# Where the sixteen matmuls of probabilities and values stand inside a slot

## The reference, cut to what matters

```python
qkv = einsum('bsh,oh->bso', hidden_states, w_qkv)      # 16 heads of 32
scores = einsum('bhqd,bhkd->bhqk', q, k) * scale
scores = where(causal, scores, finfo.min)
probs = softmax(scores, axis=-1)
attn = einsum('bhqk,bhkd->bhqd', probs, v)             # the sixteen matmuls
x = layernorm(x + einsum('bsh,oh->bso', attn, w_o))
```

## Time and profile before

| | |
|---|---|
| median of 3 runs | 2699.21 us (2698.35 to 2701.85) |
| the profiled execution | 2696.95 us, its span 2695.2 us |
| granted TensorE clock, mean | 0.992 |
| PE busy | 2629.0 us of the span, 98% |
| DVE busy | 1554.0 us, 58% |
| ACT busy | 1103.4 us, 41% |
| first and last start of the values' matmuls | 65.8 us and 735.2 us |

### The profile page before, as it was taken

One profiled execution on the slowest core, in us unless ns is written; L12 is line 12 of the kernel. 1 busy time (PEld: TensorE's weight loads), 2 busy tenths in 40 slices (PEclk: granted clock), 3 DMA queues, 4 the chain that ended last, 5 costly groups with the idle time before them and its releaser, 6 DMA issues.

```text
span 2695.2 us, 37715 instructions
## 1 busy us (share of the span) xinstructions
PE 2629.0 (98%) x13314; PEld 2146.4 (80%) x13314; DVE 1554.0 (58%) x3224; ACT 1103.4 (41%) x2518; POOL 827.1 (31%) x992
## 2 busy tenths in 40 slices
PE   7999999999789999999999999999999999999998
PEld 6777887778467888888888888888888888888886
DVE  5777777777788888876333333633333363333334
ACT  4666666666644444443222222322222232222221
POOL 1444444443633443334111111321111132111112
PEclk9999999999799999999999999999999999999999
DMA  8666876768376565556444433554344335433441
GB/s 247 186 181 174 219 211 173 190 187 234 103 257 242 195 223 213 213 203 240 174 172 174 178 141 141 196 218 172 141 173 179 141 155 225 174 141 141 178 174 47
DMA packets 143085, 493.52 MB, mean 183 GB/s; under 512 B 11568, under 2 KB 48560, under 8 KB 118320
## 3 DMA queue, kind: packets, MB, share of 16 engines
q1 hardware_dynamic: 142896, 491.11, 52.9%
HBM read 356.84 MB, written 134.22 MB: 182 GB/s over the span
## 4 chain that ended last, share of the span: by engine, by line
PE 70%; DVE 2%; DMA 1%; issue 1%; POOL 0%; ACT 0%; SPq 0%; POOLq 0%; DVEq 0%; ACTq 0%
PE bank L1035 23%; PE bank L1036 23%; PE bank L1037 23%; DMA scale<-up_scales 0%; PE bank L448 0%; DMA scale<-down_scales 0%; PE bank L434 0%; DMA x1T_scratch<-x_late 0%; POOL probs L736 0%; DVE bstats L1483 0%; DVE acc L1426 0%; DVE w_d L1399 0%; SPq L915 0%; PE bank L415 0%; PE bank L458 0%
## 5 line engine op out<-in xcount | busy, mean ns | idle before, releaser
L1645 POOL TENSOR_TENSOR inter_l<-hid,inter_h 128x512 fp32r<-128x512 f32 x256 | 339.2, 1325 | 1366.8 <-ACT inter_h L1166 1366.8
L1426 DVE TENSOR_TENSOR acc<-acc,bank 128x512 f32<-128x512 f32 x512 | 350.3, 685 | 331.6 <-PE bank L1037 322.6
L1035 PE MATMUL bank<-wd,inter_h 128*128 128x512 f32 x1024 | 399.7, 390 | 8.1 <-DVE acc L1426 7.1
L1037 PE MATMUL bank<-wd,inter_l 128*128 128x512 f32 x1024 | 398.9, 390 | 0.0
L1036 PE MATMUL bank<-wd,inter_h 128*128 128x512 f32 x1024 | 398.9, 390 | 0.0
L736 POOL TENSOR_SCALAR probs<-probs,row_inv 128x128 f32<-128x128 f32 (+3 forms) x512 | 264.5, 538 | 365.8 <-DVE row_inv L657 365.8
L1445 DVE TENSOR_TENSOR hid<-hid,bank 128x512 f32<-128x512 f32 x192 | 132.0, 687 | 398.9 <-PE bank L1037 397.2
L1035 PE MATMUL bank<-bx_h,wg 128*128 128x512 f32 x896 | 349.3, 390 | 4.2 <-ACT bank L1166 3.2
L1036 PE MATMUL bank<-bx_l,wg 128*128 128x512 f32 x896 | 348.7, 389 | 0.0
L1037 PE MATMUL bank<-bx_h,wg 128*128 128x512 f32 x896 | 348.6, 389 | 0.0
L1037 PE MATMUL bank<-bx_h,wu 128*128 128x512 f32 x896 | 348.6, 389 | 0.0
(11 more groups left out here) (139 smaller groups left out, 4355.0 us busy)
## 6 DMA issues: line engine op xcount, KB each, us to landing
wg<-w_scratch SPq DMA_DIRECT2D x48, 1792.0 KB, 9.0
wu<-w_scratch SPq DMA_DIRECT2D x48, 1792.0 KB, 12.8
wd<-w_scratch SPq DMA_DIRECT2D x48, 1024.0 KB, 4.9
q_st<-qk_scratch SPq DMA_DIRECT2D x128, 256.0 KB, 5.1
k_st<-qk_scratch SPq DMA_DIRECT2D x128, 256.0 KB, 6.9
w_scratch<-wg SPq DMA_DIRECT2D x16, 1792.0 KB, 9.6
w_scratch<-wu SPq DMA_DIRECT2D x16, 1792.0 KB, 6.0
qk_scratch<-q_stage SPq DMA_DIRECT2D x32, 512.0 KB, 3.6
```

The source lines that it names most:

```text
L1035: pe.matmul(out, a(0), b(0), start=start, stop=False, skip_group_check=True)
L1037: return pe.matmul(out, a(1), b(0), start=False, stop=stop, skip_group_check=True)
L1426: dve.tensor_tensor(a, a, d_bank[n % 2][:, :], ALU.add).then_inc(d_added, 1)
L1645: pool.tensor_tensor(inter[1][:, m, t, :], hid[:, 2 * m + t, :], f32(inter[0][:, m, t, :]), ALU.subtract).then_inc(inter_split, 1)
```

## The change

One number in the PE order: the values are issued in step k = 2 instead of step k = 0. They still stand behind that step's scores and projections and ahead of that step's transposes; the transposes of the first and the second key tile (k = 0 and k = 1) now go ahead of them.

```diff
-                        if v_head and v_head[1] % 4 == 3 and k == 0:
+                        if v_head and v_head[1] % 4 == 3 and k == 2:
                             values(t_use(b, s - 1, 0, cur, prev), v_head[0] // 4, v_head[1] // 4)
                         if t_head:
                             transpose_probs(t_use(b, s, k, cur, prev), *t_head, k)
```

## The result

The changed kernel takes 2739.8 us in the median against 2699.3 before: a ratio of 1.0147, 95% interval 1.0131 to 1.0163. The profiled execution took 2739.65 us, its span 2737.9. One of its four executions took 9388 us and is left out of the ratio. The forecast was 2740, range 2727 to 2749.

A forecast was written before the change was run, and what follows sets the result against it. PE was taken as the bound, busy 85.92 of 86.58 us in a batch. Terms 15.8 + 11.1 + 11.2 + 0 + 2.0 + 0.6 = 40.7 us, added to 2699.2, gave 2740 us; range (8 in 10) 2727 to 2749.

The forecast's parts named there:

- slots 3 and 15 and slot 11 of batch 0: Fifteen slots where third transposes and fourth score come late: 1.05 us each, 15.8 us in all.
- Slot 7: Batches 1 to 7, DVE late from an output projection: 1.59 us each, seven times, 11.1 us.
- Slot 11: Batches 1 to 6, DVE loaded by normings and x1 transposes: 1.86 us each, six times, 11.2 us.
- Odd ones: Slot 7 of batch 0: 0; batch 7: slot 11 2.0 us, slot 15 0.6; slot 3 of batch 8: nothing.
- Wait (a): Third transposes, now right behind the values, wait for DVE's copy of key tile 0: 0.85 us in slot 3.
- Wait (b): Fourth score waits for the mask behind DVE's copy of key tile 0: about 0.2 us, 1.05 later in all.
- The upper bound: 2750 us: 0.2 to 0.3 us more in each of 30 slots for PE's next weights, tail 2 more.
- Slot 11 of batch 7: No projections there; values start only behind the first mask: 0.7 to 2.8 us lost, 2.0 taken.
- ACT's delay at nothing: ACT's waiting copy delays two exponentials and a stage copy; ACT, 41% busy, stood idle there: no cost.
- No loss: Rival: no loss or a gain of 1 to 2 us if pT's space were free; 2698 us, chance 0.05.
- The direct wait alone: Rival: DVE catches up, so only the third transposes' wait for the copy costs; 2724 us, chance 0.11.
- The clock: Rival: each new wait of about 1 us also lowers PE's granted clock; 2803 us, chance 0.04.

The follow-up runs named there:

- e1: Changed kernel (values in step 2) plus a second buffer for the first head of every second group; 2703.2 us, ratio 1.0017.
- e4: Changed kernel, values still in step 2 but ahead of that step's projection matmuls instead of behind them; 2719.6 us, ratio 1.0079.
- e5: Changed kernel, but in slots with values DVE issues the second mask before the copy of key tile 0; 2732.0 us, ratio 1.0124.
- e8: Changed kernel plus the second buffer, values spread: the four matmuls of key tile k stand in step k; 2718.6 us, ratio 1.0077.
- e6: Changed kernel, but values back in step 0 in slot 11 of batch 7 only; 2735.4 us, ratio 1.0137.
- e7: As e1, but second buffer only for key tiles 0 and 2, copied by DVE; ACT's copy of key tile 1 still waits; 2709.1 us, ratio 1.0038.
- e2: Kernel before (values in step 0) plus the second buffer for the first head of every second group; 2697.8 us, ratio 1.0000.
- e3: Changed kernel with the values in step 1 instead of step 2, one buffer; 2705.0 us, ratio 1.0026.

## Why the prediction was right

*The terms.* By its own steps: slots 3 and 15 and slot 11 of batch 0, forecast 15.8, measured 15 times about 1.13, 17.0 us. Slot 7, forecast 11.1, measured 8.3. Slot 11, forecast 11.2, measured 10.4. Odd ones, forecast 2.6, measured 3.5. The sum of the slots is 39.3 against 40.7. The medians differ by 40.5 us, which is nearer to the forecast than the terms deserve: errors of both signs cancelled, and the 1.2 us between 39.3 and 40.5 belong to no term of the sum. Of the signs named, the batch came to 91.70 us against 92.1 forecast, and the waits of L434 for pT (L677) grew by 27.0 us against some 25.

*Wait (a), the third transposes:* forecast 0.85 later than before, measured 0.90 in slot 3 of batch 6 (5.81 us behind the slot's first score before, 6.71 after; the row shows 0.89 as idle time). The copy starts 0.14 behind the values' end (591.96), where 0.03 was reckoned, and the values start 3.46 behind the first score, where 3.52 was. e1 and e4 show the cause. *Wait (b), the mask behind the copy:* 0.20 forecast, 0.19 measured, of which e5 gives 0.14 to the mask. Another 0.05 comes behind the fourth score, so 1.14 in all, and e5 takes it away together with the mask's 0.14. The upper bound had allowed 0.2 to 0.3 us a slot for a PE that must take in weights behind a wait: e5 beside e1 shows no such price.

*Slot 7 was mis-sized by 0.46 us.* I read it in batch 5, and took its DVE row as the rule. There the first mask comes 0.37 us late with no releaser but "issue" (timelines of DVE, before and after):

```profile
493.25 0.29 DVE L668 CUSTOM_DVE_ANT_0 probs<-bank,mask 128x128 f32<-128x128 f32 x1 [0.37 <-issue]
518.34 0.29 DVE L668 CUSTOM_DVE_ANT_0 probs<-bank,mask 128x128 f32<-128x128 f32 x1 [0.37 <-issue]
```

That is the exception: in batch 4 after, the same mask ends at 426.57, in time for the third score at 426.63. Only batch 5 lost 1.51. A second batch would have shown it before.

*Slot 11:* the mechanism, late masks behind values that no longer cover them, was right (0.5 us by e1, none by e8).

*Slot 11 of batch 7:* 2.0 forecast within 0.7 to 2.8, measured 3.60. Two things were wrong. The sum reckoned with the first mask and left out the one before it: the second score waits 1.87 us for the last mask of slot 10, and the values start 4.85 us behind the slot's first score instead of 4.37. And 2.0 lay between values at full and at half clock; they took 4.44 us, at half clock. Where the clock rose under them (e5), the slot lost 1.79. e6 gives the slot back whole.

*ACT's delay at nothing:* with DVE's delay gone (e7) it is true in three slots and 0.35 us short in slot 11. How much of the changed kernel's own loss is ACT's, no run separates.

*The rivals.* No loss fell with the first profile, and its own condition, a free place in pT, was made in e1 and e2: even then the whole is no gain. Its gain is real only where it was read, in batch 0 (1.5 us in e1), and slot 11 costs more than that. The direct wait alone is ruled out by the 1.71 to 1.76 us of slot 11. The clock did not fall in the batches: PEclk is 1.00 in all of 91.70 us, with four waits of 0.89 in it. In the tail it was at half in places before as after.

## What to carry to other kernels

A buffer used once per group ties the last reader of one group to the first writer of the next, and the distance between them in the reader's queue is paid for or hidden by whatever stands next to it. Before a block is moved, list who waits for its end, and what stands behind that waiter in its own queue; then count the microseconds of other work left between the block and the first user of the waiter's result. A long block also fills the time in which a neighbour catches up, so a move can cost at the place that it leaves.

## What the runs showed of the hardware that was not expected

Breaking one run of 32-column matmuls into four groups between full-width ones costs 0.28 us a break (e8), though the same matmuls run and none waits.

Four waits of 0.89 us in a batch of 91.70 us left the granted clock at 1.00, and e5 beside e1 shows no further price for taking up the work again behind such a wait.

A delay of some 0.35 us on DVE with no releaser but "issue" stands at one place of the instruction stream, not of the schedule. In the kernels before and after and in e3, e4, e5 and e6 it sits ahead of the first mask in slot 7 of batch 5 (0.35 to 0.37 us), whatever the time. In the four kernels with the second buffer, e1, e2, e7 and e8, it is gone from there and sits ahead of a 512-column mask in slots 7 and 13 of batch 1 (0.31 to 0.33); in e1 the first of the two stands just ahead of the step of 0.34 us in slot 8 of batch 1. What causes it stays open.
